# Four loads of turned blocks issued behind the first weight tile of a step instead of behind its last

## The chip, the core and the metric

The kernel runs on one core of one Trainium2 chip. The metric is the time of one execution on the device in microseconds (us). The kernel before was timed three times; another execution was profiled. TensorE is called PE, its weight loads PEld, VectorE DVE, ScalarE ACT, GpSimd POOL and SyncE SP. All DMAs inside the main loop are issued by SP, in the order of its program.

## What is computed

Two batches of 512 tokens with 512 features pass through a state-space mixer with 128 heads in 8 groups, a layer norm, a feed-forward layer with folded low-rank terms, and another layer norm. The mixer is nearly all of the time:

```
proj = einsum('bsd,ed->bse', x, in_proj_w)      # gate, hs, B, C, dt
hBC  = silu(causal 4-tap conv(proj of hs, B, C))
xch  = hs * dt                                  # chunks of 128 tokens
Y_diag = einsum('bzlhn,bzshn,bhzls,bzshp->bzlhp', C, B, L, xch)
states = einsum('bzlhn,bhzl,bzlhp->bzhpn', B, decay_states, xch)
Y = Y_diag + C @ carried state + hs * D
out = group_norm(Y * silu(gate)) * norm_w @ out_proj_w.T
x = layernorm(x + out); x = layernorm(x + ffn(x))
```

## The kernel before

The 1024 tokens are 8 chunks (c = 0 to 7) of 128. Each of the 8 head groups g is cut in two halves (e = 0, 1) of 8 heads. The main loop has one step for each (g, e, c), so 16 steps in a group and 128 in all. All engines run their own program over the same steps and meet at semaphores.

In a step PE multiplies the scaled tokens `xdt` with the masked decay matrices (L725), updates the state (L735 to L737), projects the gated output (L597 to L599), and computes one, two or three **weight tiles** of the input projection for the steps ahead (L549 to L551). How many tiles a step has stands in the table `WORK`: in the first half (e = 0) steps c = 0, 1, 6, 7 have two and the others one; in the second half steps 0, 5, 6, 7 have two, step 1 has three, and 2, 3, 4 have one. In the last group the second half has only its four gate tiles, two each in steps 0 and 1.

**A weight tile's way.** SP loads it into one of the two slots of `raw` (`load_w`, L416), four tiles ahead of the step's own. ACT copies it to a rounded high part `w_hi` (L789), and POOL subtracts to get the low part `w_lo` (L1069). SP may load a slot again only when both parts of the tile two before are made: `load_w` waits for `w_hi_ready` and `w_lo_ready`. In a step with several tiles POOL makes the first `w_lo` early in the step and the next one late, behind `decay_hidden`. Behind the load of some tiles SP issues up to four loads of the output weights (`WO_LOADS`, L425).

**A chunk's way to token order.** The channels `hs` lie across the partitions, and `xdt` needs the tokens there. For chunks 1 to 7 this goes through memory. DVE turns 32x32 blocks into `x_blk` (L1290), two steps ahead. SP stores them to `turned_d` (`store_blocks`, L396), and reads them back in another order with four DMAs of 64 KB (`load_blocks`, L406) into one of two slots of `x_tok_sb`. `load_blocks` waits for the store's landing (`blocks_stored`), for the loads before (`x_here`), and for `xdt` of the chunk whose slot it takes (`xdt_ready`). POOL then waits for `x_here` and multiplies with the time steps (`scale_tokens`, L1095), in the step before the chunk's own. Chunk 0 goes through PE instead.

**POOL's order in a step** is: add the carried part to `dh` (L1146), decay the state (L1151), `w_lo` of the first tile (L1069), `scale_tokens` of the next chunk (L1095), gate of this chunk (L1205), a small power (L1210), `dh` of the next chunk (L1116), `decay_hidden` of the next chunk (`xd` L1105, `xd_hi` L1107, `xd_lo` L1109), `w_lo` of the other tiles. ACT squares the gated output (L1015) and makes its high part (L884), and DVE goes on with sums (L1497 or L1504 and L1506), the low part (L1321), `eac` (L1328), `var` (L1309), and in steps 0 and 1 the low parts of the output weights `wo_lo` (L1315). DVE masks the decay matrices once a step (L1297) after ACT's exponentials (L895).

**SP's order in a step** is: `load_eac`, `load_decay`, `store_blocks` of the chunk two steps ahead, the loads of the step's weight tiles, `load_blocks` of the chunk just stored, and in step 7 the small tables of the next unit.

Of the kernel before, what the change touches and what calls it, by code (L numbers as in the profile page):

```python
# [82 lines left out]
def wait(eng, sem, value):  # L83

    if not (isinstance(value, int) and value <= 0):
        eng.wait_ge(sem, value)
# [8 lines left out]
def mixer_ffn_kernel(nc, x_t, x_tok, w_t, unit_chan, group_chan, dt_bias, a_log, wo_t,  # L95
                     ffn_w, lora_a, lora_b, lora_w, ffn_bias, eye, upper, out):
    ctx = ExitStack()
    with ctx:
# [132 lines left out]
        def step(g, e, c):  # L231
            return g * 16 + (8 * e + c)
# [21 lines left out]
        def ahead(e, c, n):  # L254

            k = 8 * e + c + n
            return k // 16, k % 16 // 8, k % 8
# [9 lines left out]
        def turn_n(g, e, c):  # L267

            return 7 * (2 * g + e) + c
# [35 lines left out]
        def tiles_of(e, c, last):  # L305

            return [t for t in STEP_TILES[e][c] if not (last and e == 1 and t.kind != "G1")]
# [45 lines left out]
        def load_unit(q, u, slot):  # L353

            q.dma_start(tok[:, slot].rearrange("p a b c -> p (a b c)"),
                         tok_d[:, bass.ds(u, 1), :].rearrange("p o n -> p (o n)")).then_inc(unit_loaded[slot], 16)
            load_elast(q, u, slot)
# [6 lines left out]
        def load_channels(q, u, slot):  # L364
            q.dma_start(uch[:, slot, :], unit_chan[bass.ds(u, 1)].rearrange("o p n -> p (o n)")).then_inc(unit_loaded[slot], 16)

        def load_group(q, g):
            q.dma_start(gch[:].rearrange("p a b -> p (a b)"),
                         group_chan[bass.ds(g, 1)].rearrange("o p n -> p (o n)")).then_inc(group_loaded, 16)

        def load_decay(q, g, e, c):


            wait(q, yd_ready, step(g, e, c) - (1 if c % 2 else 3))
            src = acum_d[c, (2 * g + e) * UH:(2 * g + e + 1) * UH, :]
            q.dma_start(decay[:, dslot(c)].rearrange("p a b -> p (a b)"),
                        bass.AP(tensor=src.tensor, offset=src.offset, ap=[[0, P], [1, UH * P]])).then_inc(decay_loaded[dslot(c)], 16)

        def load_eac(q, g, e, c):

            wait(q, dh_ready, 0 if step(g, e, c) == 1 else step(g, e, c))
            for h2 in range(2):
                src = eacum_d[c, h2, (2 * g + e) * UT:(2 * g + e + 1) * UT, :]
                q.dma_start(eac[h2 * HD:(h2 + 1) * HD].rearrange("p a b -> p (a b)"),
                             bass.AP(tensor=src.tensor, offset=src.offset,
                                     ap=[[0, HD], [1, UT * P]])).then_inc(eac_loaded, 16)
# [3 lines left out]
        def _(sp):  # L390
            def store_blocks(g, e, c):

                n = turn_n(g, e, c)
                sp.wait_ge(blocks_turned, n)
                wait(sp, x_here, 64 * (n - 2))
                sp.dma_start(turned_d[n % 2].rearrange("i a n -> (i a) n"),  # L396
                             x_blk[:].rearrange("p q j b -> p (q j b)")).then_inc(blocks_stored, 16)

            def load_blocks(g, e, c):

                n = turn_n(g, e, c)
                sp.wait_ge(blocks_stored, 16 * n)
                wait(sp, x_here, 64 * (n - 1))
                wait(sp, xdt_ready, step(g, e, c) - 1)
                for q in range(UT):
                    sp.dma_start(x_tok_sb[q * BLK:(q + 1) * BLK, n % 2].rearrange("a i j b -> a i (j b)"),  # L406
                                 turned_d[n % 2, :, :, q * P:(q + 1) * P].rearrange("i a n -> a i n")).then_inc(x_here, 16)
# [67 lines left out]
            def load_tile(g, t, last):  # L475

                if last and t.e == 1 and t.kind != "G1":
                    return
                load_w(g, t)
                if t.n in WO_LOADS:  # L480
                    off, we, js = WO_LOADS[t.n]
                    if not (last and off) and (g + off, we) != (0, 0):
                        for j in js:
                            load_wo(g + off, we, j)
# [8 lines left out]
            def body(g, last):  # L493
                for e in range(2):
                    for c in range(8):
                        o1, e1, c1 = ahead(e, c, 1)
                        if c1 % CPB and not (last and o1) and (g, e, c) != (0, 0, 0):
                            load_eac(sp, g + o1, e1, c1)
                        od, ed, cd = ahead(e, c, 2 if c % 2 else 4)
                        if not (last and od):  # L500
                            load_decay(sp, g + od, ed, cd)
                        o2, e2, c2 = ahead(e, c, 2)
                        if c2 and not (last and o2):
                            store_blocks(g + o2, e2, c2)
                        for t in tiles_of(e, c, last):
                            off, n = divmod(t.n + 4, GRP_TILES)
                            if not (last and off):
                                load_tile(g + off, LOOP_TILES[n], last)
                        if c2 and not (last and o2):
                            load_blocks(g + o2, e2, c2)  # L510
                        if g == 0 and e == 0:
                            sp.dma_start(acc[:, c, :], x_tok[:, c, :]).then_inc(acc_loaded, 16)
                        if c == 7 and not last:
                            load_channels(sp, 2 * g + (e + 2), e)
                            load_unit(sp, 2 * g + (e + 2), e)
                        if e == 0 and c == 4 and not last:
                            load_group(sp, g + 1)
                        if last and (e, c) == (0, 7):
                            for dst, src in ((ffn_w_sb, ffn_w), (lora_a_sb, lora_a), (lora_b_sb, lora_b),
                                             (bias_sb, bass.AP(tensor=ffn_bias.tensor, offset=0, ap=[[0, P], [1, HID]])),  # L520
                                             (lw[:], lora_w)):
                                sp.dma_start(dst, src).then_inc(ffn_loaded, 16)

            groups(body)
            for t in range(CHUNKS):
                if t < CHUNKS - 1:
# [1085 lines left out]
```

## Time and profile before

| | before |
|---|---|
| time, median of 3 (lowest to highest) | 1674.83 us (1674.68 to 1677.95) |
| the profiled execution's own time | 1673.55 us |
| its span, first to last instruction | 1671.7 us |
| mean granted clock of PE | 0.986 of full speed |
| busy: PE, PEld, DVE | 1567.9, 1268.2, 1380.4 us |
| busy: ACT, POOL | 1230.5, 1376.6 us |
| DMA engines, mean busy share and rate | 45.5%, 142 GB/s |

The busy times come from the profile's first part. A matmul's end is modelled in it and neighbours overlap, so 94% busy on PE says only that PE is seldom without work; each microsecond in which it is idle is listed with the engine that ended it. The waits view names for each waiting instruction the event that came last. A timeline gives single instructions, with the idle time before them in brackets. "issue" is a wait that the profile puts down to nothing it sees.

### The profile page before, as it was taken

Reading aid. Unit: us, or ns where it says so; the run is one execution under the profiler, and the core shown is the slowest. Engines: PE = TensorE matmul, PEld = TensorE weight load, DVE = VectorE, ACT = ScalarE, POOL = GpSimd, SP = SyncE. Lnnn points to the kernel's source line nnn. Section 1 sums busy time; section 2 is a strip of 40 time slices with the busy share of each in tenths; the row PEclk is TensorE's granted clock in tenths of the full one; section 3 lists DMA queues with packets and bytes.
Section 4 is the critical chain, followed back from the end, with each engine's and each line's share of the span. In section 5 each row is a group of like instructions: output and inputs, shape, how many; then the busy total and the mean of one; then the engine's idle time right before and its main releaser. Section 6 shows DMA issues by size and latency. Waiting matters only on the chain.

```text
span 1671.7 us, 27534 instructions
## 1 busy us (share of the span) xinstructions
PE 1567.9 (94%) x8664; PEld 1268.2 (76%) x8664; DVE 1380.4 (83%) x1878; ACT 1230.5 (74%) x2391; POOL 1376.6 (82%) x1157
## 2 busy tenths in 40 slices
PE   8999998999999899999999989999998999999988
PEld 6778777877787777777777777777777777777765
DVE  6686898978978799787979879887898878978787
ACT  5798677886767776786767867877777876768764
POOL 4588788887888878898779988888798897888874
PEclk9999999999999999999999999999999999999999
DMA  3664444544454443544445443453544445354531
GB/s 111 210 197 150 149 130 150 159 127 145 124 157 144 145 131 126 168 133 147 128 123 178 133 146 116 138 177 117 157 126 154 153 127 154 109 168 140 164 113 57
DMA packets 168800, 237.45 MB, mean 142 GB/s; under 512 B 25552, under 2 KB 86992, under 8 KB 168400
## 3 DMA queue, kind: packets, MB, share of 16 engines
q1 hardware_dynamic: 167648, 235.53, 45.5%
q8 instruction: 70, 1.15, 0.3%
q14 instruction: 74, 0.61, 0.1%
q10 hardware_dynamic: 1008, 0.17, 0.1%
HBM read 201.53 MB, written 34.08 MB: 141 GB/s over the span
## 4 chain that ended last, share of the span: by engine, by line
POOL 31%; PE 21%; issue 19%; DVE 16%; ACT 8%; DMA 2%; SPq 2%; ACTq 0%; DVEq 0%; POOLq 0%
POOL y L1205 7%; DVE hs L1259 5%; PE proj L549 5%; PE proj L550 5%; PE proj L551 5%; POOL w_lo L1069 4%; POOL xd L1105 4%; POOL dh L1116 3%; POOL xd_lo L1109 3%; POOL xdt L1095 3%; POOL dh L1146 2%; DVE g_lo L1321 2%; ACT decay L877 2%; POOL xd_hi L1107 2%; DMA x_tok_sb<-turned_d 2%
## 5 line engine op out<-in xcount | busy, mean ns | idle before, releaser
L549 PE MATMUL proj<-x_hi,w_hi 128*128 128x512 f32 x1160 | 467.1, 403 | 22.1 <-issue 15.2
L550 PE MATMUL proj<-x_lo,w_hi 128*128 128x512 f32 x1160 | 457.1, 394 | 0.0
L551 PE MATMUL proj<-x_hi,w_lo 128*128 128x512 f32 x1160 | 456.5, 394 | 0.0
L1069 POOL TENSOR_TENSOR w_lo<-raw,w_hi 128x512 fp32r<-128x512 f32 x209 | 293.1, 1404 | 36.2 <-ACT w_hi L789 31.4
L877 ACT ACTIVATE decay<-decay,tok 128x128 f32<-128x128 f32 x1024 | 312.6, 392 | 0.0
L1259 DVE SCALAR_TENSOR_TENSOR hs<-proj,uch,hs 128x511 f32<-128x511 f32 (+2 forms) x384 | 283.6, 739 | 33.6 <-ACT hs L816 27.9
L549 PEld LDWEIGHTS proj<-x_hi,w_hi 128*128 128x128 f32 x1160 | 221.4, 191 | 73.7 <-issue 30.7
L551 PEld LDWEIGHTS proj<-x_hi,w_lo 128*128 128x128 f32 x1160 | 220.8, 190 | 47.1
L550 PEld LDWEIGHTS proj<-x_lo,w_hi 128*128 128x128 f32 x1160 | 221.4, 191 | 42.2
L1015 ACT ACTIVATE ysq<-y 128x512 f32<-128x512 f32 x128 | 80.6, 630 | 221.0 <-POOL y L1205 220.9
L1297 DVE TENSOR_TENSOR decay<-decay,cb 128x1024 f32<-128x1024 f32 x128 | 199.6, 1559 | 49.7 <-ACT decay L895 49.6
L1146 POOL TENSOR_TENSOR dh<-dh,eac 128x512 f32<-128x512 f32 x96 | 131.1, 1366 | 111.1 <-DVE eac L1328 111.0
L597 PE MATMUL p_out<-wo_hi,g_hi 128*128 128x512 f32 x512 | 208.0, 406 | 9.2 <-issue 4.4
L1205 POOL TENSOR_TENSOR y<-y,gate 128x512 f32<-128x512 f32 x128 | 194.9, 1522 | 11.0 <-DVE y L1446 11.0
L599 PE MATMUL p_out<-wo_hi,g_lo 128*128 128x512 f32 x512 | 202.8, 396 | 0.0
L598 PE MATMUL p_out<-wo_lo,g_hi 128*128 128x512 f32 x512 | 202.6, 396 | 0.0
L1095 POOL TENSOR_TENSOR xdt<-x_tok_sb,dt_blk 128x512 f32<-128x512 f32 x112 | 123.1, 1099 | 61.8 <-DMA x_tok_sb<-turned_d 61.8
L1116 POOL TENSOR_TENSOR dh<-hs,uch 128x512 f32<-128x512 f32 x122 | 155.8, 1277 | 0.0
L1109 POOL TENSOR_TENSOR xd_lo<-xd,xd_hi 128x512 fp32r<-128x512 f32 x96 | 135.9, 1415 | 7.7
L816 ACT ACTIVATE hs<-proj,uch 128x512 f32<-128x512 f32 x128 | 97.1, 772 | 61.2 <-PE proj L551 61.0
L725 PE MATMUL p_yd<-decay,xdt 128*64 128x128 f32 x2048 | 140.1, 279 | 1.9 <-POOL xdt L1095 1.5
L789 ACT ACTIVATE w_hi<-raw 128x512 fp32r<-128x512 f32 x197 | 122.6, 622 | 25.3 <-PE proj L551 24.1
(142 smaller groups left out, 3051.8 us busy)
## 6 DMA issues: line engine op xcount, KB each, us to landing
decay<-acum_d SPq DMA_DIRECT2D x128, 512.0 KB, 4.6
raw<-w_t SPq DMA_DIRECT2D x209, 256.0 KB, 2.9
turned_d<-x_blk SPq DMA_DIRECT2D x112, 256.0 KB, 2.5
x_tok_sb<-turned_d SPq DMA_DIRECT2D x448, 64.0 KB, 2.1
eac<-eacum_d SPq DMA_DIRECT2D x192, 128.0 KB, 3.1
wo_raw<-wo_t SPq DMA_DIRECT2D x32, 256.0 KB, 4.3
c_new<-wo_t SPq DMA_DIRECT2D x32, 256.0 KB, 4.2
hs<-x_t SPq DMA_DIRECT2D x8, 256.0 KB, 5.8
```

The source lines that it names most:

```text
L549: nc.tensor.matmul(dst[:], w_hi[:, ws, k, :], x_hi[:, k, cols], start=(k == 0), stop=False)
L550: nc.tensor.matmul(dst[:], w_hi[:, ws, k, :], x_lo[:, k, cols], start=False, stop=False)
L551: mm = nc.tensor.matmul(dst[:], w_lo[:, ws, k, :], x_hi[:, k, cols], start=False, stop=(k == KC - 1))
L597: nc.tensor.matmul(p_out[:], g_hi[:, j, :], wo_hi[:, j, :], start=(j == 0), stop=False)
L598: nc.tensor.matmul(p_out[:], g_hi[:, j, :], wo_lo[:, j, :], start=False, stop=False)
L599: mm = nc.tensor.matmul(p_out[:], g_lo[:, j, :], wo_hi[:, j, :], start=False, stop=(j == UT - 1))
L877: ins = nc.scalar.activation(decay[:, dslot(c), h, :], decay[:, dslot(c), h, :], ACT.Relu, scale=-1.0, bias=tok[:, e, 0, c, h:h + 1])
L1069: nc.gpsimd.tensor_tensor(w_lo[:, s].rearrange("p a b -> p (a b)"), raw[:, s, :], w_hi[:, s].rearrange("p a b -> p (a b)").bitcast(F32), A ...
L1116: nc.gpsimd.tensor_tensor(dh[:], hs[:, e, :, c * P:(c + 1) * P], bcast(d_skip(e), 2, P), ALU.mult).then_inc(dskip_done if c % CPB else dh_ ...
L1205: nc.gpsimd.tensor_tensor(y[:], y[:], gate[:, c // CPB, :, (c % CPB) * P:(c % CPB + 1) * P], ALU.mult).then_inc(gated, 1)
L1259: nc.vector.scalar_tensor_tensor(out=dst[:, shift:], in0=src[:, :SEQ - shift], scalar=w, in1=dst[:, shift:], op0=ALU.mult, op1=ALU.add).th ...
L1297: nc.vector.tensor_tensor(decay[:, dslot(c)], decay[:, dslot(c)], bcast(cb[:, c, :], 1, UH), ALU.mult).then_inc(mix_ready, 1)
```

## The change

The four loads of `load_blocks` are issued directly behind the load of the step's first weight tile (with the output weights that hang on that tile). The step's second and third tile come behind them. Where a step has no tile, the loads stay where they were; where it has one, the order is the same as before. What `load_blocks` itself waits for is unchanged.

```diff
-                        for t in tiles_of(e, c, last):
+                        tiles = tiles_of(e, c, last)
+                        for i, t in enumerate(tiles):
                             off, n = divmod(t.n + 4, GRP_TILES)
                             if not (last and off):
                                 load_tile(g + off, LOOP_TILES[n], last)
-                        if c2 and not (last and o2):
+                            if i == 0 and c2 and not (last and o2):
+                                load_blocks(g + o2, e2, c2)
+                        if not tiles and c2 and not (last and o2):
                             load_blocks(g + o2, e2, c2)
```

`c2` is the chunk two steps ahead; it is 0 in step 6, where there is nothing to load.

## Rows read from the trace of the kernel before

**Rows 1.** Waits of all engines, whole span: waiter, releaser, us in total, times, longest
```profile
POOL xdt L1095 <- DMA x_tok_sb<-turned_d: 61.8, 36, 4.1
```

**Rows 2.** Chain that ended last, 1245 to 1250 us: start, us, what
```profile
1245.36 0.33 SPq L416
...
1247.16 2.35 DMA x_tok_sb<-turned_d
```

**Rows 3.** Waits of all engines, 1053 to 1252 us: one group's sixteen steps
```profile
POOL xdt L1095 <- DMA x_tok_sb<-turned_d: 6.9, 4, 3.0
...
PE p_st L735 <- POOL xd_lo L1109: 4.4, 4, 1.7
...
PE p_misc L572 <- DVE var L1309: 3.1, 2, 1.6
...
PE proj L549 <- issue: 1.2, 2, 1.0
```

**Rows 4.** SP's issues, 1155 to 1184 us: start, us until the last is issued, what
```profile
1155.46 0.33 SPq L396 DMA_DIRECT2D turned_d<-x_blk  x1
1155.88 8.44 SPq L416 DMA_DIRECT2D raw<-w_t  x2
1164.43 1.95 SPq L406 DMA_DIRECT2D x_tok_sb<-turned_d  x4
...
1170.92 0.37 SPq L396 DMA_DIRECT2D turned_d<-x_blk  x1
1171.38 6.20 SPq L416 DMA_DIRECT2D raw<-w_t  x2
```

**Rows 5.** Lines L396 and L406, whole span: DMAs from issue to landing
```profile
DMA to landing us min/median/max: 2.0/2.5/6.4
...
DMA to landing us min/median/max: 1.8/2.1/4.4
```

**Rows 6.** POOL in order of time, 1164 to 1182 us; in brackets its idle time before
```profile
1164.21 1.30 POOL L1069 TENSOR_TENSOR w_lo<-raw,w_hi 128x512 fp32r<-128x512 f32 x1
1168.55 1.30 POOL L1095 TENSOR_TENSOR xdt<-x_tok_sb,dt_blk 128x512 f32<-128x512 f32 x1 [3.04 <-DMA x_tok_sb<-turned_d]
...
1180.30 1.72 POOL L1069 TENSOR_TENSOR w_lo<-raw,w_hi 128x512 fp32r<-128x512 f32 x1
```

**Rows 7.** PE in order of time, 1175 to 1183 us
```profile
1175.55 0.64 PE L735 MATMUL p_st<-xd_hi,b_hi 128*128 128x512 f32 x1 [1.72 <-POOL xd_lo L1109]
...
1182.13 0.47 PE L549 MATMUL proj<-x_hi,w_hi 128*128 128x512 f32 x1 [1.00 <-issue]
```

**Rows 8.** ACT in order of time, 1166 to 1189 us
```profile
1166.62 2.01 ACT L895 ACTIVATE decay<-decay 128x1024 f32<-128x1024 f32 x2
1171.12 0.63 ACT L1015 ACTIVATE ysq<-y 128x512 f32<-128x512 f32 x1 [2.49 <-POOL y L1205]
...
1187.91 0.63 ACT L789 ACTIVATE w_hi<-raw 128x512 fp32r<-128x512 f32 x1 [0.97 <-PE proj L551]
```

**Rows 9.** All engines in order of time, 1074 to 1088 us
```profile
1074.20 1.06 POOL L1095 TENSOR_TENSOR xdt<-x_tok_sb,dt_blk 128x512 f32<-128x512 f32 x1 [2.53 <-DMA x_tok_sb<-turned_d]
...
1077.50 0.63 ACT L1015 ACTIVATE ysq<-y 128x512 f32<-128x512 f32 x1 [1.75 <-POOL y L1205]
...
1083.12 0.46 PE L572 MATMUL p_misc<-cT,bT 128*128 128x128 f32 x2 [1.58 <-DVE var L1309]
...
1087.86 0.47 PE L597 MATMUL p_out<-wo_hi,g_hi 128*128 128x512 f32 x1 [0.74 <-issue]
```

**Rows 10.** DVE and POOL in order of time, 1102 to 1106 us
```profile
1102.40 1.05 POOL L1095 TENSOR_TENSOR xdt<-x_tok_sb,dt_blk 128x512 f32<-128x512 f32 x1 [0.58 <-DMA x_tok_sb<-turned_d]
...
1103.39 1.21 DVE L1297 TENSOR_TENSOR decay<-decay,cb 128x1024 f32<-128x1024 f32 x1
1103.41 2.35 POOL L1205 TENSOR_TENSOR y<-y,gate 128x512 f32<-128x512 f32 x1
```

**Rows 11.** Clock beside the work, one stretch (PEclk is 1.00 at full speed)
```profile
1175.76:1179.17 3.41, 3.18 (x8) 2.00 (x8) 3.08 (x3) 3.40 (x9) 3.41 (x3) 0.50 0.26 85
```

## The prediction

> **What bounds the kernel now.** I read the waits first, then the chain that ended last, then the timelines of one group of heads. PE is busy for 1567.9 of 1671.7 us, so an edit that adds no work and removes none can win at most PE's idle time, some 104 us. In group 5 (its sixteen steps lie in 1053 to 1252 us) PE waits 4.4 us for POOL's `xd_lo`, 3.1 us for DVE's `var` and 1.2 us ahead of weight tiles [rows 3]. The reader should see that these are ends of one chain that starts at POOL. POOL stands idle 61.8 us in front of `scale_tokens`, 36 times, until the loads of the turned blocks land [rows 1]. In group 5 that is 6.9 us in four waits [rows 3]. The chain that ended last runs through one of them: SP issues a weight tile (L416), then the four loads, and the last takes 2.35 us to land [rows 2].
>
> Why are these loads late? SP stores the blocks at 1155.46 us; a store lands in 2.0 to 6.4 us, in the median 2.5 [rows 4, 5], so the four loads could go at about 1158. They go at 1164.43, because SP issues two weight tiles ahead of them, 8.44 us from the first to the last [rows 4]: the second tile's slot is free only when POOL has made a late `w_lo`, which ends shortly before 1164, where it makes the next one [rows 6]. So POOL waits at 1168.55 for loads that stood behind POOL's own earlier work.
>
> **What the change moves.** Steps with two or three tiles and a chunk to load are c = 0, 1, 7 of a first half and 0, 1, 5, 7 of a second: seven a group, of which three are left in the last group (its second half has no tiles to load behind the first). That is 7 x 7 + 3 = 52 steps and 208 of the 448 DMAs. Nothing is added or taken away.
>
> *The four loads* move ahead of the second tile. Issuing them takes 1.95 us [rows 4] and each lands in 1.8 to 4.4 us, 2.1 in the median [rows 5]. Stored at 1155.46, issued from about 1158 to 1160, they are there by 1162.5, or 1165 with the slowest store. POOL is free for `scale_tokens` at 1165.51, where its `w_lo` ends [rows 6]. The wait of 3.04 us goes whole.
>
> *The second tile* now stands behind a wait for the store and the issue of four DMAs. Its cover is its own wait: it goes at about 1163.98, and the four before it are done by 1160 to 1163.8. Cost nothing. In the next step the margin is thinner: store at 1170.92, second tile at 1171.38 + 6.20 = 1177.6 [rows 4]; a store that takes 5 us lands at 1176, the loads are issued by 1177.9, so the tile may go 0.3 us late, or some 2 us once POOL runs ahead. What hides that is the distance to its use: ACT turns to that tile at 1187.91, and there it waits for PE, not for data [rows 8]. Cost nothing, up to a delay of 7 us.
>
> *Third tile and output weights* stand behind the loads only in step 1 of a second half; same cover. In step 1 of a first half the four loads of output weights stay ahead, so the blocks queue behind them; they are needed a whole step later.
>
> *What follows in SP's program* (tables, `eac`, decay, the next store) is issued up to 1.95 us earlier, since the four issues lie inside what was a wait. That helps the next store, if at all.
>
> **What each wait is worth,** on group 5.
>
> Second half, step 0: POOL is 3.04 us earlier. From `scale_tokens` at 1168.55 to the `w_lo` that ends at 1182.02 POOL runs without idle, and PE waits for it twice, 1.72 us at 1175.55 and 1.00 us at 1182.13 [rows 6, 7], with 0.2 us of a smaller wait between. Shifted by 3.04 the first goes, and the second stays: PE would start the third tile at 1179.1 instead of 1182.1. But POOL's gate now lands where DVE masks the decay matrices. At 1103.39 DVE started that 20 ns ahead of POOL's gate and took its usual 1.21 us; POOL took 2.35 us, against 1.3 for its subtraction of the same shape [rows 6, 10]. So such a collision costs POOL 1.1 us. Moved to 1165.5, `scale_tokens` and gate end at 1167.8, ACT's first exponential at 1167.6 [rows 8]: the mask falls on the POOL instruction behind. I take 1.1 less, with 0.3 us given back because `scale_tokens` itself was slowed (1.30 against 1.05 us) [rows 6, 10]: **2.3 us**, ends 2.1 and 3.0.
>
> First half, step 0: POOL waits 2.53 us, but ACT's square stood idle only 1.75 us for it, and behind that DVE's chain runs to `var`, on which PE waits 1.58 us, and to the output weights, 0.74 us more [rows 9]. The lesser counts: **1.75 us**, ends 1.0 (a collision) and 2.3.
>
> First half, step 2: wait 0.58 us, and the gate behind it is the slowed one of 2.35 us [rows 10]. **0.6 us**; ends 0 and 1.6, if POOL now goes first.
>
> Second half, step 6: what is left of 6.9, **0.8 us**; ends 0 and 1.8.
>
> The Trainium skill (SBUF — State Buffer, "Who interferes with whom") says that a DVE instruction with two SBUF inputs and a POOL instruction that reads SBUF exclude each other, whoever comes second waiting. The 20 ns case agrees. By that rule alone the ends in which POOL comes first would be as likely as the others.
>
> **The sum.** 2.3 + 1.75 + 0.6 + 0.8 = 5.45 us a group, 43.6 us for eight. The first group's step 0 is not moved (its load stands ahead of the loop), 1.75 less; the last group has no wait in step 6 of its second half, 0.8 less, and in its step 0 the large feed-forward operands come ahead of the next store, 0.5 to 1 less. That leaves 40.4 us: 1673.55 - 40.4 = 1633.2. The median of the three runs lies 1.3 us above the profiled execution, so I say 1634.
>
> Ends: all lower ends are 3.1 us a group, about 22 us in all; all upper ends are 8.7, cut by the 6.9 waited plus what collisions give back, about 58 us.
>
> **Rivals.** *The clock takes part of it back* (inside the range). PE ran at half clock, 1.2 GHz, from 1175.76 to 1179.17 [rows 11], right behind its 1.72 us wait. That cost 1.7 us of work, most of it hidden by the wait at 1182.13. After the change one wait of about 1.7 us is left in that place and little behind it: if the clock then falls for the same 3.41 us, 1.7 us are paid in full, in seven groups 12 us: 1646. The opposite, no fall at all, brings 1620 to 1630.
>
> *The waits move on, little is won.* POOL and DVE are busy for over 1376 us each, and the two collide. If the freed time is eaten by the next wait in most places, only the second half's step 0 counts, with its clock: some 10 us, 1664. Against it speaks that POOL has no other idle time between the two waits of PE.
>
> *Nothing.* If the second tile set the pace and not the blocks, the time stays at 1674.8. Against: ACT waits for PE ahead of that tile [rows 8].
>
> *Slower: the second tile comes late.* SP now sits at the store's landing with the tile behind it. It decides where the landing plus 1.95 us comes more than 7 us after the tile's slot is free, about 13 us behind the store; the slowest seen is 6.4 [rows 5]. If stores stretched that far, and each of the 52 steps lost 1 us beyond that point, the gain of 40 would turn into a loss of 12: 1686.
>
> The Trainium skill (DMA: Bandwidth & Descriptors, "Queues, rings and completion order") says that each DMA engine takes its queue's descriptors in order, so blocks issued behind five weight loads land behind them. No row above shows a block load in that place; by the rule it would land a few us later than 2.1 and still be a step early.
>
> **Chances.** Forecast with its clock and collision cases, 1614 to 1656: 0.80. Little is won, 1656 to 1671: 0.09. Nothing: 0.04. Slower: 0.06. More than 60 us won: 0.01. The likeliest is 1634, and the range 1614 to 1656. A measurement of this kernel tells 0.2% (3.3 us) from no change. Faster by more: 0.90; within: 0.04; slower: 0.06.
>
> **What would show it.** POOL's wait for `x_tok_sb` should fall from 61.8 to under 12 us (the first load and those of one-tile steps stay); PE's waits for `xd_lo` and `var` by two thirds; the second tile's issue should not be later against `w_lo`, and ACT should not wait for `raw`. A group of sixteen steps should take some 5.5 us less. Wrong: `x_tok_sb` waits gone and PE's idle time as before (another chain was as long), a longer mean of POOL's gate (collisions), or a lower mean clock.

## The result, and the profile after

The changed kernel takes 1613.96 us (median of 4 runs, 1612.55 to 1615.98) where the kernel before, run beside it, takes 1674.76: a ratio of 0.9635, with an interval of 0.9617 to 0.9654, or 60.8 us less. The forecast was 1634, its range 1614 to 1656: the direction was right, the gain was half as large again as forecast, and the time lies just below the range. Its profiled execution took 1615.2 us. Two single executions of kernels below, 5394.2 us of step7_only and 3922.1 us of ahead_of_all, stand so far from all others that every comparison and every range leaves them out.

Lines of the kernel behind the change are three higher than before: `scale_tokens` (`xdt`) is L1098, the gate L1208, `xd` L1108, `xd_lo` L1112, the mask of the decay matrices L1300, PE's `p_st` L738, its products with weight tiles (`proj`) L552.

The page of the changed kernel, parts 1 and 2: span, busy time by engine, granted clock in tenths of full speed.

```profile
span 1613.4 us, 27534 instructions
...
PE 1547.2 (96%) x8664; PEld 1257.2 (78%) x8664; DVE 1401.1 (87%) x1878; ACT 1227.9 (76%) x2391; POOL 1380.6 (86%) x1157
...
PEclk9999999999999999999999999999999999999999
```

The row of the clock says nothing here: a tenth is too coarse for it. The summary of the cores has its mean, and it rose from 0.986 to 0.998.

```profile
core 0: 1613.4 us, clock 0.998
```

Two lines split the 58.3 us that the span lost. PE's idle time (span less busy) fell from 103.8 to 66.2 us, by 37.6. PE's **busy** time fell too, from 1567.9 to 1547.2 us, by 20.7, for the same 8664 matmuls: that is time at half clock (1 - 0.986 of 1671.7 is 23.4 us, 1 - 0.998 of 1613.4 is 3.2).

The waits of the changed kernel, whole span (waiter, releaser, us in total, times, longest):

```profile
ACT ysq L1018 <- POOL y L1208: 161.6, 73, 7.2
...
POOL dh L1149 <- DVE eac L1331: 112.8, 46, 5.1
...
PE p_st L738 <- POOL xd_lo L1112: 16.3, 19, 2.2
...
PE proj L552 <- issue: 12.6, 9, 1.9
...
PE p_misc L575 <- DVE var L1312: 8.8, 7, 1.3
...
ACT w_hi L792 <- DMA raw<-w_t: 7.7, 6, 2.1
...
POOL xdt L1098 <- DMA x_tok_sb<-turned_d: 6.2, 3, 3.7
```

POOL's wait for the turned blocks fell from 61.8 us in 36 times [rows 1] to 6.2 in 3. PE's waits for `xd_lo` and for `var` halved (31.7 and 20.1 us before). ACT now waits for a weight tile 6 times, two of them before 72 us; the kernel before had one such wait, of 1.1 us.

SP's issues in the changed kernel, 1116 to 1137 us, at the seam between the halves of group 5 (start, us until the last is issued, what):

```profile
1116.62 0.33 SPq L396 DMA_DIRECT2D turned_d<-x_blk  x1
1117.04 0.38 SPq L416 DMA_DIRECT2D raw<-w_t  x1
1118.68 1.74 SPq L406 DMA_DIRECT2D x_tok_sb<-turned_d  x4
1125.15 0.35 SPq L416 DMA_DIRECT2D raw<-w_t  x1
...
1128.80 0.37 SPq L396 DMA_DIRECT2D turned_d<-x_blk  x1
1129.27 0.38 SPq L416 DMA_DIRECT2D raw<-w_t  x1
1134.37 1.75 SPq L406 DMA_DIRECT2D x_tok_sb<-turned_d  x4
1136.21 0.38 SPq L416 DMA_DIRECT2D raw<-w_t  x1
```

The loads go 2.1 us behind the store instead of 9.0 [rows 4]. In the next step they go 5.6 us behind it, and the second tile follows at once: there the four DMAs do stand in its way, by half a microsecond at most (POOL's `w_lo` that frees its slot ends at 1135.66).

The same stretch on POOL (in brackets idle time before; none has any):

```profile
1125.37 1.29 POOL L1072 TENSOR_TENSOR w_lo<-raw,w_hi 128x512 fp32r<-128x512 f32 x1
1126.63 1.04 POOL L1098 TENSOR_TENSOR xdt<-x_tok_sb,dt_blk 128x512 f32<-128x512 f32 x1
1127.64 1.29 POOL L1208 TENSOR_TENSOR y<-y,gate 128x512 f32<-128x512 f32 x1
...
1129.89 2.02 POOL L1108 TENSOR_TENSOR xd<-xdt,tok 128x512 f32<-128x512 f32 x1
...
1138.80 1.71 POOL L1072 TENSOR_TENSOR w_lo<-raw,w_hi 128x512 fp32r<-128x512 f32 x1
```

The wait of 3.04 us [rows 6] is gone. From the start of `scale_tokens` to the end of the third tile's `w_lo` POOL took 13.88 us, before 13.47 (1168.55 to 1182.02) [rows 6]: 0.41 us net went back, as `xd` took 2.02 us (1.09 before) and `scale_tokens` and `xd_lo` less than before. DVE's mask, which took 1.2 us where nothing met it, lies over that place:

```profile
1128.85 2.17 DVE L1300 TENSOR_TENSOR decay<-decay,cb 128x1024 f32<-128x1024 f32 x1 [2.55 <-ACT decay L898]
```

So POOL is 3.04 - 0.41 = 2.63 us earlier.

The same on PE. What remains are a small wait and one ahead of the third tile:

```profile
1135.26 0.47 PE L738 MATMUL p_st<-xd_hi,b_hi 128*128 128x512 f32 x1 [0.30 <-DVE eac L1331]
...
1140.60 0.47 PE L552 MATMUL proj<-x_hi,w_hi 128*128 128x512 f32 x1 [1.65 <-issue]
```

**By steps.** I cut the span where PE begins a chunk's first `p_yd`. Groups 1 to 6 took 198.8 to 201.5 us each and take 192.0 to 194.1, on average 8.0 us less; the first saves 3.3 and the last 6.7. All of the 8.0 lies in a few steps. The table separates them into steps without half clock and the rest, since a stretch at half clock sits in one step of a group and not in the same one of the next ("without" leaves out steps in which such a stretch lengthened the step, or shortened it: see below the table).

| PE's step, groups 1 to 6 | before to after, mean us | without half clock | forecast (ends) |
|---|---|---|---|
| second half, 1 (term "second half, step 0") | 24.77 to 21.89 | 24.25 to 21.56: 2.7 | 2.3 (2.1 to 3.0) |
| first half, 1 ("first half, step 0") | 16.19 to 14.29 | 16.95 to 14.29: 2.7 | 1.75 (1.0 to 2.3) |
| first half, 2 and 4 ("first half, step 2") | 24.23 to 22.56 | 1.25 | 0.6 (0 to 1.6) |
| second half, 7 ("second half, step 6") | 13.56 to 11.74 | 12.93 to 11.74: 1.2 | 0.8 (0 to 1.8) |
| first half, 6 | 12.27 to 12.62 | -0.35 | none |
| sum of a group | 8.0 | 7.5 | 5.45 (3.1 to 8.7) |

A stretch at half clock can be paid back. In the kernel before, three of these groups have one in step 7 of the second half, which lengthens that step by 1.3 us on average. Behind two of the three, step 1 of the next first half took 14.64 and 14.72 us and POOL waited there 1.2 and 1.3 us for its blocks; the four groups without a stretch ahead took 16.70 to 17.41 us, with POOL waits of 2.5 to 4.1 us. Steps 7, 0 and 1 together took 40.1 us with such a stretch twice and 42.5 once, against 40.8 to 42.4 without one. The second trace of the kernel before (before_look) shows the same: 14.64 to 14.86 us behind four of five such stretches. So these stretches cost the kernel before next to nothing.

So of a group's 8.0 us some 7.5 are shorter waits, and 0.5 is clock (the 20.7 us of busy time above were mostly hidden by waits or paid back, so their removal did not shorten the span by as much).

### The profile page after: what moved, and what is told of

Its sections match the earlier page's. It is cut to its first block, busy times and chain, and to the rows that moved or that the text cites. A ratio compares the mean times of both kernels' runs of the same rounds, so it can differ in the third digit from the quotient of the medians.

```text
span 1613.4 us, 27534 instructions
## 1 busy us (share of the span) xinstructions
PE 1547.2 (96%) x8664; PEld 1257.2 (78%) x8664; DVE 1401.1 (87%) x1878; ACT 1227.9 (76%) x2391; POOL 1380.6 (86%) x1157
## 4 chain that ended last, share of the span: by engine, by line
PE 56%; DVE 13%; issue 12%; ACT 9%; POOL 8%; DMA 1%; SPq 0%; ACTq 0%; DVEq 0%; POOLq 0%
PE proj L552 11%; PE proj L554 11%; PE proj L553 11%; ACT decay L880 4%; PE p_out L600 4%; PE p_out L602 4%; PE p_out L601 4%; PE p_st L609 3%; PE p_yd L728 3%; DVE hs L1262 3%; DVE g_lo L1324 2%; ACT decay L898 2%; DVE ysq L1507 1%; DVE acc L1338 1%; ACT w_hi L792 1%
## 5 line engine op out<-in xcount | busy, mean ns | idle before, releaser
L552 PE MATMUL proj<-x_hi,w_hi 128*128 128x512 f32 x1160 | 463.5, 400 | 19.8 <-issue 12.6
L552 PEld LDWEIGHTS proj<-x_hi,w_hi 128*128 128x128 f32 x1160 | 219.5, 189 | 66.6 <-issue 23.7
L1300 DVE TENSOR_TENSOR decay<-decay,cb 128x1024 f32<-128x1024 f32 x128 | 211.0, 1648 | 49.0 <-ACT decay L898 48.9
L601 PE MATMUL p_out<-wo_lo,g_hi 128*128 128x512 f32 x512 | 199.6, 390 | 0.0
L1208 POOL TENSOR_TENSOR y<-y,gate 128x512 f32<-128x512 f32 x128 | 174.0, 1360 | 11.1 <-DVE y L1449 11.1
L1119 POOL TENSOR_TENSOR dh<-hs,uch 128x512 f32<-128x512 f32 x122 | 163.6, 1341 | 0.0
L1108 POOL TENSOR_TENSOR xd<-xdt,tok 128x512 f32<-128x512 f32 x96 | 147.9, 1540 | 0.3 <-DVE xdt L1275 0.2
L1449 DVE TENSOR_TENSOR y<-p_yd,dh 128x512 f32<-128x512 f32 x128 | 87.7, 685 | 63.7 <-POOL dh L1149 45.0
```

The costliest lines, as they stand in the source:

```text
L552: nc.tensor.matmul(dst[:], w_hi[:, ws, k, :], x_hi[:, k, cols], start=(k == 0), stop=False)
L601: nc.tensor.matmul(p_out[:], g_hi[:, j, :], wo_lo[:, j, :], start=False, stop=False)
L1208: nc.gpsimd.tensor_tensor(y[:], y[:], gate[:, c // CPB, :, (c % CPB) * P:(c % CPB + 1) * P], ALU.mult).then_inc(gated, 1)
L1300: nc.vector.tensor_tensor(decay[:, dslot(c)], decay[:, dslot(c)], bcast(cb[:, c, :], 1, UH), ALU.mult).then_inc(mix_ready, 1)
```

## The experiments

Two theories of the result stood against each other. By the first, POOL's waits are all of it: the sites of the forecast gave more than their middle values. By the second, a good part is PE's clock, which falls to half behind some of PE's waits, and the change removed the waits that did it. A third question was how far the loads could still be moved, and a fourth, why the parts don't add up to the whole. In every kernel below the time stands against the kernel before on the same chip.

**One part alone.** Only step 7 of each half issues early; those loads serve `scale_tokens` of the next half's step 0.

```diff
+                        early = c == 7
 ...
-                            if i == 0 and c2 and not (last and o2):
+                            if i == 0 and early and c2 and not (last and o2):
                                 load_blocks(g + o2, e2, c2)
-                        if not tiles and c2 and not (last and o2):
+                        if not (tiles and early) and c2 and not (last and o2):
```

> The four loads move ahead of the second tile only in step 7 of each half; in all other steps they stay behind the last tile. They feed POOL's first scale_tokens of the next half, the waits of 2.5 and 3.0 us. Theory A (each wait counts by its own term, and a PE wait that goes takes its half-clock stretch with it): step 1 of the first half shortens by 1.9 us and step 1 of the second by 2.9, about 4.8 us a group, 34 us in all: 1641 us, 1634 to 1648; the waits for x_tok_sb fall from 61.8 to about 20 us. Rival B (moving only these runs into the next late load, that of chunk 2, which is still behind its second tile): under 15 us, above 1660. Rival C (these two waits were all that mattered): 1614 to 1620.

Measured: 1634.4 to 1640.6 us (three executions), ratio 0.978 (0.9757 to 0.9803), some 36.8 us less. The same kernel once more, for its trace:

> The loads moved in step 7 only, for an undisturbed trace. Step 1 of the first half 1.9 us shorter than before and step 1 of the second 2.9; POOL's waits for x_tok_sb at 20 us or below if only the waits of steps 2 and 6 are left, above 20 if chunk 2 is now late.

It took 1635.4 us. POOL's waits for the blocks are down to 20.1 us, 19 times, and PE's step 1 of a first half takes 14.58 us, of a second 21.98, as in the changed kernel; steps 4 (12.37) and 7 (13.18) are near the kernel before. Clock 0.994. So this part carries the first two terms of the forecast.

**The other part alone**, every step but 7:

```diff
-                        early = c == 7
+                        early = c != 7
```

> The mirror of the run before: the loads move in steps 0, 1 and 5, and stay behind the last tile in step 7. Theory A: step 4 of the first half shortens by up to 1.5 us and step 7 of the second by up to 1.8, 2.5 to 3.3 us a group, 18 to 25 us in all: 1650 to 1657. The forecast's terms for these two places (0.6 and 0.8 us a group) give 10 us: 1665. Rival C (only step 7 matters): 1672 to 1677. PE's waits in step 1 of the second half stay, and with them half-clock stretches there.

Measured: 1658.3 us (1655.6 to 1661.4), 0.991 (0.9892 to 0.9928), 16.4 us less. Step 4 is 11.33 and step 7 is 11.52 us, as in the changed kernel, and the steps 1 keep their waits (17.00 and 25.02). The clock stays at 0.987: the long waits that are left still pull it down. 36.8 + 16.4 = 53.2 us against 60.8 for the whole. By the intervals of the three ratios each of these numbers is known to 3 or 4 us, so the gap of 7.6 is not much more than noise. By the profiled executions it is 5.0 us of span (38.1 + 15.2 against 58.3): the parts take 23.3 + 10.1 us off PE's idle time and the whole 37.6, and 13.6 + 1.9 us off the time at half clock, the whole 20.2.

**Clock without any shorter wait.** The kernel before, with 134 matmuls whose product nobody reads (30.5 us of PE work), put into PE's waits. The loads stay late.

```diff
+            def fill(n):
+                for _ in range(n):
+                    nc.tensor.matmul(p_hid[:].rearrange("p a b -> p (a b)"), x_hi[:, 0, 0:P], x_hi[:, 0, 0:SEQ], start=True, stop=True)
 ...
+                            if g and (e, c) in ((1, 1), (0, 4)) and not ffn_step:
+                                fill(5 if e else 3)
                             pe.wait_ge(xd_ready, updates(g, e, c))
```

(5 more stand ahead of the wait for `var` in step 1 of a first half, and 2 and 6 ahead of the second and third tile of the second half.)

> The order of the kernel before, with PE given work that nobody needs in places where it waits: 5 matmuls of 0.23 us in step 1 of a first half, 3 in step 4, and 5, 2 and 6 ahead of its three waits in step 1 of a second half; 134 in all, 30.5 us. No wait of any other engine changes. Theory D (idle PE makes the clock fall, and that costs time of its own): half-clock stretches in these places go, from 47.5 us in all to about 20, and the time falls by 3 to 10 us, 1665 to 1672. Rival E (the clock is a bystander, its stretches are hidden by the next wait): 1674 to 1680, the fill's own work where it overlaps.

Measured: 1669.5 us (10 runs, 1665.1 to 1672.9), 0.9969 (0.9954 to 0.9985). With more work PE is done 5.2 us earlier, so the clock has a price of its own in the kernel before. It is a small one beside the 60.8. Its busy times on its page, and the line of its clock in the summary of the cores:

```profile
PE 1592.1 (95%) x8798; PEld 1287.5 (77%) x8798; DVE 1377.1 (83%) x1878; ACT 1230.3 (74%) x2391; POOL 1375.1 (82%) x1157
```

```profile
core 0: 1668.2 us, clock 0.990
```

PE's busy time less the 30.5 us of filling is 1561.6, 6.3 less than before. The steps tell where that counts. Step 1 of a second half took 24.24 to 24.37 us in groups 1 to 6, without any half clock. In the kernel before it took 24.18 to 24.40 in four of these groups, although three of them had a stretch at half clock, and 25.82 in the other two. In the three the stretch followed PE's first wait, and the wait ahead of the third tile hid it, as forecast from [rows 7, 11]. In the two it followed the last wait, and the step took 1.6 us longer. One of the two, kernel before, PE:

```profile
974.49 0.50 PE L735 MATMUL p_st<-xd_hi,b_hi 128*128 128x512 f32 x1 [1.71 <-POOL xd_lo L1109]
...
981.07 0.65 PE L549 MATMUL proj<-x_hi,w_hi 128*128 128x512 f32 x1 [1.85 <-issue]
981.52 0.63 PE L550 MATMUL proj<-x_lo,w_hi 128*128 128x512 f32 x1
```

**Ahead of all tiles.** The four loads go directly behind the store, in the kernel before:

```diff
+                        if c2 and not (last and o2):
+                            load_blocks(g + o2, e2, c2)
                         for t in tiles_of(e, c, last):
 ...
-                        if c2 and not (last and o2):
-                            load_blocks(g + o2, e2, c2)
```

> The four loads go directly behind the store, ahead of the first tile as well, in every step, so every weight tile stands behind a wait for the store's landing and four issues. The slower rival of the forecast put the point from which that costs at 7 us of delay. First tiles are now issued 4 to 7 us later and are used 9 us behind their landing. Theory: 1613 to 1620, ACT's waits for raw stay under 20 us. Rival (tiles have less slack than I read): 1 us a step and more, above 1700.

Measured: 1657.0 to 1664.6 us (three executions), 0.9923 (0.9898 to 0.9948), some 46 us slower than the change. The expectation was wrong. The waits and SP's and ACT's timelines of this kernel (lines as in the kernel before):

```profile
ACT w_hi L789 <- DMA raw<-w_t: 77.2, 35, 4.9
...
POOL xdt L1095 <- DMA x_tok_sb<-turned_d: 7.5, 4, 4.0
```

```profile
1157.85 0.37 SPq L396 DMA_DIRECT2D turned_d<-x_blk  x1
1162.99 1.74 SPq L406 DMA_DIRECT2D x_tok_sb<-turned_d  x4
1164.83 0.85 SPq L416 DMA_DIRECT2D raw<-w_t  x2
```

```profile
1167.47 0.63 ACT L789 ACTIVATE w_hi<-raw 128x512 fp32r<-128x512 f32 x1 [2.30 <-DMA raw<-w_t]
```

POOL's waits are gone here too. But the **first** tile of step 1 now stands behind the store's landing (5.1 us) and the four issues, and ACT wants it at 1165.2 us: it waits 2.30 us for it. Step 1 of a first half took 16.81 us with 2.45 of PE idle, of a second 23.97. So the slower rival of the forecast is real and some microseconds away: in the change the first tile stays ahead, and ACT's waits for tiles are 7.7 us in all.

**Another order on POOL.** In the changed kernel PE's wait ahead of the third tile (1.65 us) comes behind `dh`, the decay of the state and `w_lo` on POOL. Here, in step 1 of a second half, `w_lo` of the third tile goes ahead of the decay of the state.

```diff
-                        if c % CPB in (1, 2):
-
+                        def decay_state():
 ...
+                        late_state = (e, c) == (1, 1) and not last
+                        if c % CPB in (1, 2) and not late_state:
+                            decay_state()
 ...
                             if nxt:
                                 split_lo(g + nxt[0], nxt[1])
+                            if i == 0 and late_state:
+                                decay_state()
```

> The changed kernel, and in step 1 of the second half POOL makes the third weight tile's w_lo ahead of the decay of the state instead of behind it (seven groups). In the changed kernel PE still waits 1.65 us there for that w_lo, and the decay takes 1.5 us. Theory: that wait goes, nothing waits for the later state (PE needs it a tile and a projection later): 1.5 us a group, 10 us in all, 1602 to 1608. Rival (POOL's later operations or the next step's gate set the pace): 1612 to 1616.

Measured: 1613.5 us (1612.9 to 1614.2), 0.9642 (0.9625 to 0.966), the same as the changed kernel. PE in this kernel, where the 1.65 us were:

```profile
1133.69 0.47 PE L552 MATMUL proj<-x_hi,w_hi 128*128 128x512 f32 x1 [0.34 <-ACT w_hi L792]
...
1137.10 0.47 PE L552 MATMUL proj<-x_hi,w_hi 128*128 128x512 f32 x1 [0.41 <-issue]
```

The wait broke into smaller ones, 1.50 us in that step instead of 1.98: the step takes 21.51 us, and without half clock it takes 21.56 in the changed kernel. A miss of the expectation. PE's idle time in the step fell by 0.5 us and its length by 0.05; what took the place of that wait wasn't looked for.

**Why the parts don't add up.** Everything moved but steps (0,0), (1,0) and (1,1), which serve chunk 2 and 3 of a half.

```diff
+                        early = (e, c) not in ((0, 0), (1, 0), (1, 1))
```

> The loads move in steps 7, in step 1 of the first half and in step 5 of the second. In step 0 of both halves and step 1 of the second they stay behind the last tile; the kernel before had no wait in front of what these feed. The forecast took them for free and worth nothing: 1612 to 1616. Rival: once POOL runs 2 to 3 us earlier it meets the loads of chunk 2, which are then the late ones, and that is the 7.6 us by which the two part moves together (36.8 + 16.4) fall short of the whole (60.8): 1619 to 1624, with new waits of POOL for x_tok_sb in step 1 of both halves, 8 to 15 us in all.

Measured: 1622.1 us (1616.3 to 1622.8), 0.9686 (0.9664 to 0.9708). POOL's waits for the blocks are 8.0 us in 4 times against 6.2 in 3, so those steps hardly wait: the time lies in the range of the rival, but not by its mechanism. PE's idle time is 65.7 us, that of the changed kernel 66.2; the clock is 0.993, not 0.998. Its PE (lines one higher than in the changed kernel), group 4, and the clock of that stretch (window, length, busy us and count of PE, PEld, DVE, ACT, POOL, PEclk, DMA share, GB/s):

```profile
951.58 0.47 PE L553 MATMUL proj<-x_hi,w_hi 128*128 128x512 f32 x1 [1.86 <-issue]
951.89 0.39 PE L554 MATMUL proj<-x_lo,w_hi 128*128 128x512 f32 x1
...
952.40 0.63 PE L553 MATMUL proj<-x_hi,w_hi 128*128 128x512 f32 x1
952.83 0.63 PE L554 MATMUL proj<-x_lo,w_hi 128*128 128x512 f32 x1
```

```profile
952.30:955.70 3.40, 3.40 (x9) 2.62 (x9) 1.57 (x2) 0.96 (x2) 3.40 (x4) 0.50 0.74 233
```

The wait ahead of the third tile is 1.86 us here, not 1.65, and behind it PE runs at 1.2 GHz for 3.4 us: the matmuls start 0.43 us apart instead of 0.23. That happened in 4 of the 6 middle groups (all six have that wait at 1.85 or 1.86), in the changed kernel in one (755.5 us, behind its only wait of 1.86; the other five are 1.65). Such a stretch adds 1.6 us: the step takes 23.56 or 23.57 us with it and 21.99 and 22.01 without. The longer wait alone adds 0.4 (21.56 in the changed kernel). Another call of the changed kernel itself, below, took 1620.3 us with waits of this kind in four groups, a ratio of 0.9678 (0.9653 to 0.9703). So it isn't shown that leaving these steps late costs anything.

The kernel before once more, for a second trace:

> The kernel before once more, for a second trace of the same program: how much of its time hangs on where the half-clock stretches fall. If the clock costs time of its own, span minus PE's idle time minus half of the half-clock time is the same in both traces within 3 us, and the number of the stretches (12 of 3.41 us or longer in the first) need not be.

1676.5 us, clock 0.984. As expected, PE's busy time less what half clock takes is the same within 1 us (1545.0 and 1544.5), with three stretches more. The clock of the kernel before moves a little from run to run, and stays far from that of the changed one.

**Filling that wait.** The kernel of the last paragraph but one, with 6 matmuls that nobody reads ahead of the tile of B in the second half (seven groups, 9.6 us of work):

```diff
                             for t in todo:
+                                if t.kind == "B" and not ffn_step:
+                                    fill(6)
                                 project(g, t)
```

> The order of all_but_step0, with 6 matmuls that nobody needs (1.37 us) in PE's last wait of step 1 of the second half, in front of the third tile; no other engine is touched. Its trace had the same idle time of PE as the changed kernel (60.5 against 61.0 us) and 14.8 us more at half clock, all in this step, behind a wait of 1.86 instead of 1.65 us. Theory D (the clock alone makes its 6 to 8 us): the half-clock stretches of this step go and the time comes down to 1613 to 1617 although PE has 9.6 us more to do. Rival E (something else in that step is slower): 1621 to 1627.

1615.7 us (1615.2 to 1616.6), 0.9651 (0.9626 to 0.9675), some 6 us less than unfilled, though the two intervals touch. The trace is clearer: clock 0.997, idle 57.0 us, busy 1556.5, no stretch in these steps, and they take 21.54 to 22.02 us. The same filling in the changed kernel:

> The changed kernel with the same 6 matmuls that nobody needs in front of the third tile in step 1 of the second half. Theory D: no half-clock stretch in that step, whatever the wait there is (1.65 or 1.87 us), so the time is that of the changed kernel in its better trace or a little below, 1611 to 1616 us or a ratio of 0.962 to 0.965, at 9.6 us more of PE's work. Rival E: the ratio of the changed kernel's second look, 0.968 or above.

1616.0 us (1614.1 to 1616.1), 0.9637 (0.9601 to 0.9673), clock 0.998.

**Lengthening it.** The changed kernel with one 128x128 copy on POOL that nobody reads, ahead of the first `w_lo` in step 1 of a second half (7 in all):

```diff
+                            if i == 0 and (e, c) == (1, 1) and not last:
+                                nc.gpsimd.tensor_copy(scrap[:], ident[:])
                             if nxt:
                                 split_lo(g + nxt[0], nxt[1])
```

> The changed kernel with one small copy on POOL (128x128, some 0.35 us) ahead of the first w_lo of step 1 of the second half, in seven groups. PE's wait of 1.65 us there grows to 2.0. Theory D: half-clock stretches come back in most groups, each 1.7 us: 2.5 us for the wait and 7 to 12 us for the clock, 1623 to 1629. Rival E: the wait alone, 1616 to 1618.

Beside it on the same chip, the changed kernel:

> The changed kernel once more, on the chip of the two runs beside it: 1612 to 1617 us, under 15 us at half clock.

With the copy 1627.6 us (1626.6 to 1629.9), 0.9719 (0.969 to 0.9749); the changed kernel there 1620.3 (1618.8 to 1622.1), 0.9678 (0.9653 to 0.9703). The expectation for the changed kernel was missed by some 3 us, and its half clock is 25 us, not under 15. The copy holds POOL for 0.75 us, and not for the 0.35 of the expectation: seven times, 5.3 us in all. It cost 7.3. So the price of the wait alone could be up to 5.3 us, and the times by themselves hardly tell the theories apart; the two traces do. They are 10.0 us apart, of which 4.6 are idle time of PE and 5.0 half clock. The copies, and one of the stretches, PE:

```profile
L1162 POOL COPY scrap<-ident x7: 749/751/754, 176.2 to 1341.5; 128x128 f32<-128x128 f32 x7
```

```profile
954.77 0.77 PE L553 MATMUL proj<-x_hi,w_hi 128*128 128x512 f32 x1 [2.35 <-issue]
955.33 0.63 PE L554 MATMUL proj<-x_lo,w_hi 128*128 128x512 f32 x1
```

Five of the six middle groups have such a stretch (clock 0.990), three in the changed kernel beside it (0.993), where the waits are 1.65 to 1.88 us. And the changed kernel itself takes 1614.0 us in one call and 1620.3 in another: the same program, with one of these stretches in the middle groups or with three. The filled kernels, one call each, took 1615.7 and 1616.0. None is faster than the changed kernel at its best.

All profiled executions side by side (step7_only's was the one of 5394 us; busy less lost is PE's busy time less the part lost at half clock, (1 - clock) x span, and less the unneeded matmuls):

| kernel | span | PE idle | clock | busy less lost |
|---|---|---|---|---|
| before | 1671.7 | 103.8 | 0.986 | 1544.5 |
| before_look | 1674.7 | 102.9 | 0.984 | 1545.0 |
| fill_before | 1668.2 | 76.1 | 0.990 | 1544.9 |
| not_step7 | 1656.5 | 93.7 | 0.987 | 1541.3 |
| ahead_of_all | 1655.2 | 99.6 | 0.995 | 1547.3 |
| step7_look | 1633.6 | 80.5 | 0.994 | 1543.3 |
| changed_plus_copy | 1628.1 | 69.8 | 0.990 | 1542.0 |
| all_but_step0 | 1620.1 | 65.7 | 0.993 | 1543.1 |
| changed_again | 1618.1 | 65.2 | 0.993 | 1541.6 |
| step0_late_filled | 1613.5 | 57.0 | 0.997 | 1542.1 |
| changed (after) | 1613.4 | 66.2 | 0.998 | 1544.0 |
| changed_filled | 1612.3 | 55.7 | 0.998 | 1543.8 |
| swap_state | 1611.5 | 62.6 | 0.998 | 1545.7 |

The last column holds within 6 us through all of them. So the span of this kernel is a fixed amount of PE work, plus PE's idle time, plus what half clock takes. The last two aren't independent: where a wait follows, time at half clock only stands in place of idle time.

## Why the prediction was right and wrong

**Right: what bounds the kernel and what the change frees.** POOL stood in front of the loads, and the chain from there to PE's waits gave the time back. Of the signs named, the blocks' waits are 6.2 us (under 12 forecast), and group 5's loads are issued 2.1 us behind their store, with POOL without idle time. PE's waits for `xd_lo` and `var` fell by 49% and 56%, less than the two thirds forecast. ACT waits for `raw` four times in step 1 of a second half, where the forecast had none; PE's idle time in those four groups is 5.6 us each, in the other two middle groups 5.8 and 5.6, so these waits cost nothing that shows.

**Wrong: the sum sized the waits too small.** This is the step that failed. The four terms were 2.3, 1.75, 0.6 and 0.8 us a group and measured 2.7, 2.7, 1.25 and 1.2; less 0.35, which PE waits longer for `xd_lo` in step 6 of a first half (1.13 us, before mostly 0.92, twice 0.47), that is 7.5 instead of 5.45 us. Over the six middle groups it makes 12.3 of the 18.0 us between the forecast for the profiled execution, 1633.2, and its 1615.2. Group 5, on which the terms were worked out, shows it by itself: 199.2 to 192.1 us, so 7.1, and its one stretch at half clock had been hidden.

The term most out is the first half's step 0, outside its own ends. "The lesser counts" capped it at the 1.75 us that ACT's square stood idle. But PE lost 2.32 us there, in two waits (1.58 and 0.74), and has no wait left in that step. The cap left out that POOL's gate was itself slowed before and no longer is, since it now starts ahead of DVE's mask. The gate and the mask, kernel before and changed kernel:

```profile
1074.84 1.50 DVE L1297 TENSOR_TENSOR decay<-decay,cb 128x1024 f32<-128x1024 f32 x1 [1.59 <-ACT decay L895]
1075.21 2.26 POOL L1205 TENSOR_TENSOR y<-y,gate 128x512 f32<-128x512 f32 x1
```

```profile
1037.47 1.29 POOL L1208 TENSOR_TENSOR y<-y,gate 128x512 f32<-128x512 f32 x1
...
1039.66 1.70 DVE L1300 TENSOR_TENSOR decay<-decay,cb 128x1024 f32<-128x1024 f32 x1 [1.60 <-ACT decay L898]
```

The forecast had a collision as this term's lower end, so as something to come, and not as something that was there. The low part on DVE (L1321, now L1324) took 1.35 us and takes 0.67 in that place. In the first half's step 2 of group 5 POOL's gate now comes first too (1.30 us against 2.35), the upper case of the forecast. In the second half's step 0 the mask did fall on what stands behind the gate, as forecast, but POOL lost 0.41 us net where the sum had 0.8.

**Wrong too, but smaller: the clock stood beside the sum instead of in it.** The profiled execution of the kernel before had a clock of 0.986, so 23.4 us of PE's time went to half clock. The prediction looked at one stretch out of twelve, found its cost hidden by the next wait, and carried the clock only as a rival inside the range, with 1620 to 1630 as its best. The trace bears it out in most places of the middle groups: three stretches in step 1 of a second half were hidden, and of three in step 7 two were more than paid back, as said below the table of steps. Two lay behind the wait ahead of the third tile and cost 1.6 us each, and one in the first half's step 4 made that step some 2.5 us longer and step 6 0.5 shorter. After the change one is left, with 2.0 us. That makes some 3 us in the six groups. The last group saved 6.7 where the forecast had 3.9, with two stretches gone there, and what part of that is clock isn't known; the first saved 3.3 for 3.7. Together 12.3 + 3 + 2.8 - 0.4 = 17.7 us of the 18.0. fill_before is of that order: with 6.7 us less lost to half clock (23.4 to 16.7) the kernel before took 5.2 us less. So the first of the two theories accounts for most of what the forecast lacked, and the clock for the smaller part.

**The other side of that rival,** that the remaining wait of about 1.7 us would pull the clock down in seven groups (1646), came true in part: it didn't happen behind waits of 1.65 us, and did behind most of the longer ones. The changed kernel sits at this edge, hence 1614 in one call and 1620 in another.

**The range** had a lower end where all terms take their upper values at the clock of before, 58 us, and gave more than 60 us a chance of 0.01. Terms above their middle and a better clock together were left out, though both follow from the same cause, shorter waits.

**Slower, nothing, little:** the second tile was late by half a microsecond in one step of a group, with the distance to its use to cover it. ahead_of_all shows what the mechanism costs once the first tile is hit: 46 of the 61 us. The Trainium skill (DMA: Bandwidth & Descriptors, "Queues, rings and completion order") has the blocks behind the weight loads of the same queue land behind them. The traces agree. In step 1 of a first half the blocks now stand behind five such loads, and in their median they land 3.9 us after their issue, before 2.3; in step 1 of a second half they no longer stand behind two loads of output weights and a further tile, and it is 1.9 us, before 3.7. The four loads of one such first half, changed kernel:

```profile
L406 SPq DMA_DIRECT2D x_tok_sb<-turned_d x4: 371/424/432, 669.3 to 670.7; - x4
...
DMA to landing us min/median/max: 3.6/3.8/4.3
```

They are needed a step later, as the forecast said, and POOL waits for none of them. Over all blocks the median is 1.9 us, before 2.1 [rows 5], which hides this.

**Contention between POOL and DVE.** By the Trainium skill (SBUF — State Buffer, "Who interferes with whom") either can be the one that waits, and the runs agree: the gate got faster (194.9 to 174.0 us in total), and DVE's mask slower (199.6 to 211.0). The prediction's "usual 1.21 us" of the mask is its time where nothing meets it; its median over the kernel before is 1.49.

## What to carry to other kernels

Moving loads ahead of work that waits for something else is worth it where the consumer stands idle behind its own earlier work; leave ahead of them the one transfer whose consumer has the least time. In a kernel bound by PE, make (1 - clock) x span a term of the sum, list every stretch at half clock and what hides it or pays it back in the steps behind, and expect waits and clock to move together. Before a wait is taken as the measure of a term, look whether the instruction behind it was slowed by another engine, and whether it still will be. When two parts of a change don't add up, compare PE's idle time and its clock before looking for another wait.

## What the runs showed of the hardware

The wait ahead of the third tile, in the six middle groups of five kernels (changed, changed_again, all_but_step0, changed_plus_copy, step7_look), and whether PE's granted clock fell to 1.2 GHz for 3.4 us behind it: behind waits of 1.65 to 1.67 us in none of 11, of 1.85 to 1.88 us in 9 of 13, of 2.10 to 2.36 us in 5 of 6. Most of the longer waits have another of 0.3 us some 5 us ahead, so the length of the one wait need not be what decides. With 0.2 us more of waiting the same step takes 0.4 us longer, and 2.0 where the clock falls too (21.56, 22.0 and 23.6 us). PE work that nobody needs, put into that wait, cost nothing in the changed kernel and saved some 6 us in all_but_step0. What the clock goes by beyond that, these runs don't tell: in the kernel before it fell behind waits of 1.71 and 1.72 us in three groups, and held behind one of 1.92 and one of 1.85 in group 2.

A stretch at half clock in step 7 of a second half was followed by a step 1 that was some 2 us shorter, in 9 of 11 cases of the three traces with all loads late (before, before_look, fill_before). Behind stretches at the same place in step7_look, where those loads are early, that step took 14.2 to 15.2 us, against 14.3 without: there was no wait left that could shrink.
